# Attention's steps ordered chunk by chunk, and the first batch's stacks loaded by halves

## The reference

```
c_q = x @ W_DQ                    # x is the normed input, latent width 64
Q   = concat(c_q @ W_UQ, rope(c_q @ W_QR))        # 16 heads, 16 + 8 wide
K   = concat(c_kv @ W_UK, rope(x @ W_KR))         # the rope part is shared by all heads
scores = clip(Q K^T, -80, 80), causal mask
attn   = softmax(scores / sqrt(24)) @ V           # V = c_kv @ W_UV, 16 wide
out    = attn @ W_O
```

## Time and profile before

| | us |
|---|---|
| median of three runs | 2783.69 |
| the profiled execution | 2781.41 |
| its span, first to last instruction | 2779.7 |
| span until the first score matmul | 82.7 |
| attention's steps of 8 batches | 82.7 to about 990 |

### The profile page before, as it was taken

How to read it: one execution, slowest core, us unless ns; L and a number is a source line. 1 busy time by engine, 2 the same in 40 slices (tenths; PEclk the granted TensorE clock), 3 DMA queues, 4 the chain that set the end, 5 groups by cost and what they waited for, 6 DMA issues and landing times. The chain is left out here.

```text
span 2779.7 us, 43055 instructions
## 1 busy us (share of the span) xinstructions
PE 2544.2 (92%) x16024; PEld 1787.8 (64%) x16024; DVE 2272.2 (82%) x3931; ACT 1929.6 (69%) x3075; POOL 621.5 (22%) x424
## 2 busy tenths in 40 slices
PE   3799899998999958999999999999999999999997
PEld 2233334333333336887888878888888887888997
DVE  4578887888877778798898889889988998887555
ACT  1687787877878836666676676666676767665886
POOL 2113121231212211111211121111111111110676
PEclk8899999999999978999999999999999999999999
DMA  3652644626445410000000000000000000001442
GB/s 99 87 97 72 103 96 84 106 69 105 93 86 95 114 46 1 1 16 16 1 16 16 8 8 16 16 1 16 16 16 1 16 16 9 1 8 51 136 137 76
DMA packets 125346, 136.75 MB, mean 49 GB/s; under 512 B 17122, under 2 KB 105186, under 8 KB 125140
## 3 DMA queue, kind: packets, MB, share of 16 engines
q1 hardware_dynamic: 125140, 134.00, 21.5%
HBM read 87.56 MB, written 46.40 MB: 48 GB/s over the span
## 5 line engine op out<-in xcount | busy, mean ns | idle before, releaser
L542 ACT ACTIVATE probs<-psum_a 128x1024 f32<-128x1024 f32 (+3 forms) x768 | 599.8, 816 | 210.7 <-PE psum_a L901 207.8
L1607 PE MATMUL psum_f<-w,picked 128*128 128x256 f32 (+1 forms) x2304 | 721.4, 346 | 0.0
L1606 PE MATMUL psum_f<-w,picked 128*128 128x256 f32 x2304 | 623.7, 288 | 1.2 <-DVE picked L1409 1.2
L1607 PEld LDWEIGHTS psum_f<-w,picked 128*128 128x128 f32 x2304 | 446.9, 194 | 53.4
L1606 PEld LDWEIGHTS psum_f<-w,picked 128*128 128x128 f32 x2304 | 447.3, 194 | 1.4 <-DVE picked L1409 1.4
L901 PE MATMUL psum_a<-q_stack,k_stack 72*128 72x512 f16 (+3 forms) x1536 | 378.4, 336 | 38.3 <-DMA q_stack<-q_rope_scratch 18.2
L618 DVE TENSOR_SCALAR probs<-probs 128x2048 f32<-128x2048 f32 (+3 forms) x320 | 320.1, 1000 | 84.9 <-ACT probs L542 84.8
L1234 ACT ACTIVATE gates<-psum_f 128x256 f32<-128x256 f32 (+1 forms) x384 | 186.1, 486 | 241.5 <-PE psum_f L1607 239.4
L916 PE MATMUL psum_a<-probs,v 128*17 128x512 f32 (+3 forms) x3072 | 334.2, 508 | 14.0 <-DVE probs L618 7.5
L1409 DVE TENSOR_TENSOR picked<-hid,masks 128x512 fp32r<-128x512 f32 x512 | 335.3, 715 | 13.1 <-PE psum_f L1607 10.0
L901 PEld LDWEIGHTS psum_a<-q_stack,k_stack 72*128 72x128 f16 x1536 | 98.2, 99 | 369.2 <-ACT probs L542 209.0
(11 more groups left out here) (298 smaller groups left out, 5373.8 us busy)
## 6 DMA issues: line engine op xcount, KB each, us to landing
heads_scratch<-kq_parts SPq DMA_DIRECT2D x64, 256.0 KB
k_stack<-heads_scratch SPq DMA_DIRECT2D x96, 128.0 KB
q_stack<-heads_scratch SPq DMA_DIRECT2D x96, 128.0 KB
x_in<-x_dram SPq DMA_DIRECT2D x8, 1024.0 KB, 5.5
x_res<-x_dram SPq DMA_DIRECT2D x16, 512.0 KB, 5.9
xs<-x_scratch SPq DMA_DIRECT2D x16, 512.0 KB, 3.9
xf_scratch<-xs SPq DMA_DIRECT2D x16, 512.0 KB, 2.9
xf<-xf_scratch SPq DMA_DIRECT2D x16, 512.0 KB, 6.1
```

Source lines behind the costliest of these rows:

```text
L542: act.activation(probs[:, s % PROB_SETS, 2 * u:2 * u + 2, q0:512], psum[:, 2 * u:2 * u + 2, q0:512], ACT.Exp, scale=exp_scale).then_inc(ex ...
L1606: pe.matmul(soft_out, x, cols[:, 1], start=start, stop=stop)
L1607: return pe.matmul(gate_out, x, cols[:, 2] if it == 0 else cols[:, 0::2], start=start, stop=stop)
```

## The change

The steps of a batch are ordered by chunk first: 16 steps with chunk 0 of groups 0, 1, 2, 3 (four diagonal quads), then 32 steps with chunk 1 of groups 0 to 3 (a full and a diagonal quad each). The numbering of the sums (`gci`) and the waits follow. The tables of jobs by tick stay. In batch 0 the stacks are loaded by halves of the tokens: when scratch half 0 has landed, SP loads columns 0 to 511 of group 0 (12 DMAs), then those of groups 1 to 3 together (12 DMAs), and likewise after half 1. These loads stand in SP's program right after write_scratch(0, half), the first of them ahead of the load of `x_in`. The other batches load as before, each group released by the last step of its chunk 1.

```diff
-    steps = [(g, c, j) for g in range(GROUPS) for c in range(CHUNKS) for j in range(4 * c + 4)]
+    steps = [(g, c, j) for c in range(CHUNKS) for g in range(GROUPS) for j in range(4 * c + 4)]
...
-            def load_stacks(b, g):
-
-                if b > 0:
-                    sp.wait_ge(scores_ready, 2 * ((b - 1) * STEPS + last_step[CHUNKS * g + CHUNKS - 1] + 1))
-                hs = slice(4 * g, 4 * g + 4)
+            def stack(b, first, count, cols, done):
+                hs = slice(4 * first, 4 * (first + count))
...
-                        sp.dma_start(dst[row:row + dh, hs, :],
-                                     heads_dram[b % 2, f, part, 64 * g:64 * g + 64, :].rearrange("(h r) n -> r h n", r=dh)).then_inc(stacked[g], 16)
+                        sp.dma_start(dst[row:row + dh, hs, cols],
+                                     heads_dram[b % 2, f, part, 64 * first:64 * (first + count), cols].rearrange("(h r) n -> r h n", r=dh)).then_inc(done, 16)
...
+            def load_first_stacks(half):
+
+                sp.wait_ge(scratch_written, 16 * SCRATCH_DMAS * (half + 1))
+                cols = slice(512 * half, 512 * half + 512)
+                stack(0, 0, 1, cols, first_stacked[half][0])
+                stack(0, 1, GROUPS - 1, cols, first_stacked[half][1])
+
+            def load_stacks(b, g):
+
+                sp.wait_ge(scores_ready, 2 * ((b - 1) * STEPS + last_step[GROUPS * (CHUNKS - 1) + g] + 1))
+                stack(b, g, 1, slice(0, SEQ), stacked[g])
...
                 if after < BATCH:
                     write_scratch(after, 0)
+                if after == 0:
+                    load_first_stacks(0)
                 if after + 1 < BATCH:
                     sp.wait_ge(job_done, number[("XT", after, 1, 1)] + 1)
                     sp.dma_start(x_in[:], x_v[after + 1]).then_inc(x_loaded, 16)
...
                 if after < BATCH:
                     write_scratch(after, 1)
+                if after == 0:
+                    load_first_stacks(1)
+                if 0 < after < BATCH:
                     sp.wait_ge(scratch_written, 16 * SCRATCH_DMAS * 2 * (after + 1))
                     for g in range(GROUPS):
                         load_stacks(after, g)
...
                 if kind == "OT":
-                    pe.wait_ge(attn_ready, ACCS * b + CHUNKS * (GROUPS - 1) + half + 1)
+                    pe.wait_ge(attn_ready, ACCS * b + GROUPS * (half + 1))
...
-                if u == 0 and (c, j) == (0, 0):
-                    pe.wait_ge(stacked[g], 16 * STACK_DMAS * (b + 1))
+                if u == 0 and j == 0 and b == 0:
+                    pe.wait_ge(first_stacked[c][min(g, 1)], 16 * STACK_DMAS)
+                if u == 0 and (c, j) == (0, 0) and b > 0:
+                    pe.wait_ge(stacked[g], 16 * STACK_DMAS * b)
```

More of the change, by code:

```diff
@@ L183, in attention @@
     ALL_ACCS = BATCH * ACCS
-    last_step = [max(s for s in range(STEPS) if steps[s][:2] == divmod(ci, CHUNKS)) for ci in range(ACCS)]
+    last_step = [max(s for s in range(STEPS) if steps[s][:2] == (ci % GROUPS, ci // GROUPS)) for ci in range(ACCS)]
     def last_tick(gci):
@@ L297, in attention @@
         stacked = [sem(f"stacked{g}") for g in range(GROUPS)]
+        first_stacked = [[sem(f"first_stacked{half}{i}") for i in range(2)] for half in range(2)]
         scores_ready = sem("scores_ready")
@@ L341, in write_scratch @@
                 cols = slice(512 * half, 512 * half + 512)
-                if b >= 2:
+                if b == 2:
+                    for i in range(2):
+                        sp.wait_ge(first_stacked[0][i], 16 * STACK_DMAS)
+                        sp.wait_ge(first_stacked[1][i], 16 * STACK_DMAS)
+                if b > 2:
                     for g in range(GROUPS):
-                        sp.wait_ge(stacked[g], 16 * STACK_DMAS * (b - 1))
+                        sp.wait_ge(stacked[g], 16 * STACK_DMAS * (b - 2))
                 sp.wait_ge(pool_step, POOL_STEPS_HALF * (2 * b + half + 1))
@@ L361, in load_stacks @@
                         row = i * (dh + dr)
[L362 to L363 removed]
+                        sp.dma_start(dst[row:row + dh, hs, cols],
+                                     heads_dram[b % 2, f, part, 64 * first:64 * (first + count), cols].rearrange("(h r) n -> r h n", r=dh)).then_inc(done, 16)
                 for i, part in enumerate(K_ORDER):
                     row = i * (dh + dr) + dh
[L366 to L367 removed]
+                    src = k_rope_dram[b % 2, part, :, cols]
+                    sp.dma_start(k_stack[row:row + dr, hs, cols],
+                                 src.unsqueeze(1).to_broadcast([dr, 4 * count, cols.stop - cols.start])).then_inc(done, 16)
                 for i, part in enumerate(Q_ORDER):
                     row = i * (dh + dr) + dh
[L370 to L371 removed]
+                    sp.dma_start(q_stack[row:row + dr, hs, cols],
+                                 q_rope_dram[b % 2, part, 32 * first:32 * (first + count), cols].rearrange("(h r) n -> r h n", r=dr)).then_inc(done, 16)
+            def load_first_stacks(half):
[6 more added lines that the diff above has]
+                stack(b, g, 1, slice(0, SEQ), stacked[g])
             def load_residual(b, half):
@@ L907, in weigh @@
                 b, (g, c, j) = s // STEPS, steps[s % STEPS]
-                gci = b * ACCS + g * CHUNKS + c
+                gci = b * ACCS + c * GROUPS + g
                 q0 = 128 * max(0, j - 4 * c)
```

2 lines of the change are left out of this document (1 added, 1 removed).

## The result

The changed kernel takes 2796.41 us (median of six runs, 2789.34 to 2802.34), the kernel before on the same chip 2781.88 (six runs, 2780.39 to 2785.09). The ratio of after to before is 1.005, with a 95% interval of 1.0032 to 1.0067: 14.5 us, 0.5%, **slower**. The forecast was 2781, no difference; the time lies inside the range of 2767 to 2804, but on the side that had a chance of 0.27. The profiled execution took 2794.78 with a span of 2793.0, against 2779.7.

The account below looks back on a forecast made before the run. No engine was taken as full in the steady state; ticks take turns in what limits them. Terms +0.3 - 4.8 - 1.3 + 2.8 = -3.0 us took the median from 2783.7 to about 2781, range 2767 to 2804.

Parts of the forecast that it names:

- The start: Stretch up to batch 0's first scores: stack wait goes, the wait for x_in takes its place, +0.3 us.
- The halves' prize: PE's 18.24 us wait for a stack DMA before the first scores, at which the halved loads aim.
- The chain behind it: From x_in landing at 77: 5.2 us to PE's first scores, first weigh at 88.6.
- the half set: First 24 stack DMAs of batch 0, half the bytes: about 25 us, ending near 75.
- Batch 0: First batch, without OR, norm or row statistics of y: about -1.3 us of PE.
- Ticks 0 to 15: In batches 1 to 6: ticks 4 to 8 give -1.5 us, tick 13 +0.7, together -0.8 a batch.
- the divide's 0.7: Tick 13 gains a divide with nothing to cover it: +0.7 us a batch.
- Ticks 24 to 39: Four quads of each batch, stepped at +1.6, -1.65, +0.2, -0.2: about 0, bound 1 us each way.
- Late refills: Stacks of groups 1 to 3 needed earlier in a batch: 0.4 us on each of 7 batches, +2.8.
- (c): Rival: steady state loses by divide at 13, late refills or full steps beside KR and LAT; 2790 to 2796, chance 0.15.
- (a): Rival: queue lets x_in through early, first scores at 70, -13 us, 2767; chance 0.13.
- (b): Rival: half-length rows cost what full ones do, x_in lands at 99, about 2803; chance 0.10.

Follow-up runs that it names:

- the run with each half by itself: Changed kernel with x_in loaded first, order by chunk in batch 0 alone, and own DMAs and semaphore for each group's half: 2765.25 us.

## Why the prediction was wrong

**The start: mechanism right, size short.** The halves' prize is cancelled by `x_in` behind them in the queue. Moving that one load gains 15.0 us with the order by chunk and 11.5 with the order by group in batches 1 to 7. The chain behind it was sized well: from the landing to the first scores 5.1 us (5.2 predicted), to the first weigh 11.6 (11.6). The term that was too small is the half set: it has landed at 77.8, 29.0 us after its first issue at 48.8, for which I had put 25; `x_in` follows 2.5 us behind it, for which I had put 2. So `x_in` lands at 80.3 for 77, the earlier start giving 1.2 back. I had scaled the full set's 47 us by the bytes. It is not the shorter rows that made the set slower, since with the same rows in 48 DMAs it took 23.6, even behind `x_in`; the slowness goes with the packing into 24 larger ones.

The Trainium skill, "SBUF — State Buffer", section "The DMA setup-cost knee", gives each transfer a fixed cost of some 2 us. Here the 24 DMAs of the half set and the load behind them took 31.5 us in all, so that cost overlapped, as the prediction read it; and 48 DMAs with the bytes of those 24 were in sooner, not later.

**Batch 0: wrong sign.** I gave it -1.3 and it took +4.4. Of the order, ticks 4 to 7 give -1.8 and ticks 24 to 39 +1.7. The other 4.5 us are in ticks 0 to 3 (+1.0), 8 to 15 (+2.1), 16 to 19 (+1.2) and small sums. PE's clock was at the half from 56.9 to 97.8, in before from 57.2 to 91.3, and fell again at 111 and at 132, where before has one fall at 98. The wait of 21.5 us sits right ahead of the first steps in place of one of 18.2, with DVE's catching up behind it; I had costed work and waits and nothing for the clock. That the clock makes up the 4.5 us is argued from where its falls lie, not shown. In the run with each half by itself the clock was back at 74 and batch 0 took 109.1 in the same order.

**Ticks 0 to 15: right.** -0.67 for -0.8. Ticks 4 to 8 gave -1.56 for the -1.5 worked out, and ticks 12 to 15 grew by 0.63 for the divide's 0.7. The second is less certain than it looks: between runs in the same order ticks 8 to 15 vary from 25.4 to 25.9 with the place of the clock's fall.

**Ticks 24 to 39: the step that failed.** Predicted 1.6 - 1.65 + 0.2 - 0.2 = 0 a batch; measured, in undisturbed batches, 1.93 - 1.14 + 0.64 - 0.08 = +1.35, outside the bound of 1. The step through ticks 24 to 27 was close, 0.3 short. In the two others I took ACT for the one that sets the pace. At ticks 28 to 31 I let PE's QR and KH "fit beside light steps" and put the quad at ACT's 8.1 us. PE is busy 8.61 of 8.61 us there, in every undisturbed batch, and ACT 6.22: PE sets this quad, and 0.5 of the gain was not to be had. At ticks 32 to 35 I had 9.8 to 10 us on ACT, and the quad takes 10.39. DVE is busy for 10.35 of them, and I had not counted it; but it isn't what I missed. Batch 6 has no `x_row_stats`, and its quad in the changed kernel takes as long with DVE busy for 8.47:

```profile
866.16:876.56 10.40, 9.47 (x65) 3.67 (x65) 8.47 (x9) 9.68 (x14) 3.41 (x3) 1.00 0.39 129
```

ACT first waits 0.59 us for PE and then has no gap for 10.1 us, so it was the right engine, and that wait is the nearest reading of the missing 0.4; it was not tested. With batches 3 and 6, which carry a fall of the clock in ticks 24 to 31, and batch 6's quick quad of before, the term is +2.09 a batch, +12.5 us in all. It is the largest part of the miss; 8.1 of it is the order's own and 3.3 are the falls.

**Late refills: a cost that didn't come.** I gave +2.8; in the changed kernel no step of batches 1 to 7 waits for a stack. That was luck as much as judgement. In the same order the kernel with `x_in` first waits 3.37 us in batch 7, the order alone 2.17 in batch 2 and 1.42 in batch 7, and the order with groups 0 and 1 swapped up to 2.13 in a batch.

The sum by its terms, against the prediction's -3.0: the start +2.3 more, batch 0 +5.7 more, ticks 0 to 15 +0.8 more, ticks 24 to 39 +12.5 more, refills 2.8 less, the rest of the layer 1.7 less and small sums 0.5 less: +13.3. Of the rivals, (c) had the sign and came nearest in time, with 2790 to 2796, but not by its causes: the full steps beside KR and LAT took 0.3 us a batch more than stepped, and the divide at 13 and the refills were not it. (a)'s 2767 is about what the loads give once `x_in` goes first and each half has its own DMAs, which agrees by number and not by mechanism. (b)'s mechanism, a cost per row, would have put `x_in` at 99 and is out.

**What stays open.** The order costs 6.7, 7.3 and 10.8 us by three pairs of runs. The quads' own sums give +0.7 a batch, 4 us in six. The other 3 to 7 us are not one thing. Between the two runs with `x_in` first, batches 1 to 6 differ by only 1.9 us in the profiles and batch 7 by 6.1. And in the same order batches 1 to 6 take 695.6 us in one execution, 51.2 of them at the lower clock, and 703.1 in two others, with 61.4 and 68.3 at it. Most of that difference lies in quads whose work is the same and in which a fall of the clock lies: ticks 24 to 31 of batches 3 and 6, 22.1 us for 20.4, and ticks 40 to 43 of the same two batches, 9.9 and 9.8 for 8.7 and 8.6. So falls of the clock account for this part, but what decides in which ticks they come was not found, and so neither whether the order brings them.

## What to carry to other kernels

A load that is moved earlier in a queue that serves in order is paid for by the one it overtakes: find the overtaken load's first reader before halving anything. Before packing several parts into fewer DMAs with one completion, measure when the set has landed: here the fewer and larger DMAs were the slower ones. For a new order of work, list the busy time of every engine in each stretch under the new order, not only that of the engine which seems near its limit. Then look for a stretch in which one engine's extra job is absent, since an engine can be busy for 10.35 of 10.39 us and not set the pace. And where pace is set by turns, judge a change by the sum over neighbouring stretches: shorter copies in the order of before gave 0.84 us in one quad and lost 0.82 in the next.

## What the runs showed of the hardware

- PE's clock is part of the price of an order. An unchanged quad took 13.01 us at a mean granted clock of 0.84 and 11.12 at 1.00 with the same 84 matmuls; and the rest of the layer, whose instructions are the same in all kernels, took 1785.4 to 1797.2 us in their profiled executions, with 139 us at the lower clock in the shortest and 166 in the longest. The Trainium skill, "TensorE: Matmul & The Clock Gate", section "What's actually happening", says that the gate is set by how busy PE has been recently; the falls after PE's waits for DVE agree.
- Issuing a DMA can hold the issuing engine: a small write behind 24 stack DMAs and a load of 1 MB held SP for 9.00 us. Behind 48 stack DMAs with the same bytes, `x_in` ahead of them, it took 0.30.
- More and smaller DMAs can be faster: 2.4 MB to 16 and 8 partitions at a time took 29.7 to 32.1 us in 24 DMAs and 21.6 to 23.6 in 48, in three runs each and each time behind a load of 1 MB in the same queue.
